# One product of states with C, issued as two operations with a signal each, in a hybrid attention, FFN and state-space kernel

## The reference, cut to what matters

```
def step(h, inputs):
    dt, bt, ct, xt_ = inputs
    decay = jnp.exp(A[None] * dt[:, :, None])
    inp = dt[:, :, None] * xt_[:, :, None] * bt[:, None, :]
    h = decay * h + inp
    y = jnp.einsum('bdn,bn->bd', h, ct)
    return (h, y)
```

## Time and profile before

| what | value |
| --- | --- |
| median of 3 runs | 1912.14 us (1906.36 to 1922.38) |
| profiled execution | 1914.16 us, with a span of 1912.4 us |
| granted TensorE clock, mean | 0.973 of full speed |
| busy: PE, DVE, ACT, POOL | 89%, 88%, 73%, 58% of the span |
| DMA engines | about 0.86 busy in a frame of the middle |

### The profile page before, as it was taken

The page is one execution under the profiler, slowest core; times in us unless marked ns, Lnnn a source line. Parts: engine busy times, 40 slices in busy tenths (PEclk is TensorE's granted clock), DMA queues, the critical chain, the costliest instruction groups (busy, mean ns, idle before and its releaser), DMA issues.

```text
span 1912.4 us, 31526 instructions
## 1 busy us (share of the span) xinstructions
PE 1704.7 (89%) x9578; PEld 1009.6 (53%) x9620; DVE 1678.1 (88%) x3928; ACT 1397.9 (73%) x2724; POOL 1117.4 (58%) x903
## 2 busy tenths in 40 slices
PE   6999788999989898999999898999999898888875
PEld 2555454646556564646555564646465564545333
DVE  5653889999999999999999999999999999977893
ACT  3666767797887978797887978787886968675541
POOL 2000565767667676767667676757667575766330
PEclk9999899999999999999999999999999999989998
DMA  5322586988879788979889787988878687761120
GB/s 144 91 59 75 118 170 137 186 159 169 166 148 193 153 183 149 192 159 170 165 158 185 156 186 151 184 159 176 156 161 182 144 172 145 149 128 50 55 62 11
DMA packets 216330, 275.30 MB, mean 144 GB/s; under 512 B 37169, under 2 KB 129122, under 8 KB 216162
## 3 DMA queue, kind: packets, MB, share of 16 engines
q1 hardware_dynamic: 155682, 163.17, 35.1%
q0 software_dynamic: 60480, 110.13, 34.8%
HBM read 128.49 MB, written 34.08 MB: 85 GB/s over the span
## 4 chain that ended last, share of the span: by engine, by line
PE 39%; DVE 23%; DMA 12%; issue 10%; POOL 9%; ACT 6%; SPq 1%; DVEq 0%; POOLq 0%; ACTq 0%
DVE hc L1274 10%; DMA y<-hc 8%; POOL inp L1448 6%; PE bank L422 5%; PE bank L624 5%; DVE bank L1130 4%; PE bank L541 4%; PE bank L641 3%; PE bank L486 3%; DVE hc L1282 3%; PE bank L508 3%; PE bank L625 2%; PE bank L433 2%; DMA sk<-qk_parts 1%; PE bank L604 1%
## 5 line engine op out<-in xcount | busy, mean ns | idle before, releaser
L1448 POOL TENSOR_TENSOR inp<-u,b_all 128x1024 f32<-128x1024 f32 x240 | 574.2, 2393 | 326.8 <-DVE hc L1274 123.1
L1274 DVE TENSOR_TENSOR_SCAN hc<-dec,inp 128x1024 f32<-128x1024 f32 x256 | 586.0, 2289 | 33.5 <-POOL inp L1448 13.4
L1130 DVE CUSTOM_DVE_ANT_0 bank<-bank,mask_qk 128x512 f32<-128x512 f32 (+3 forms) x1024 | 477.7, 508 | 77.8 <-PE bank L486 75.3
L915 ACT ACTIVATE pt<-bank 128x512 f32<-128x512 f32 x640 | 382.6, 608 | 108.1 <-PE bank L524 58.2
L1458 POOL DMA_DIRECT2D y<-hc x420 | 370.9, 954 | 132.8 <-DMA y<-hc 84.1
L1031 ACT ACTIVATE dec<-dt,a_neg 128x511 f32<-128x511 f32 x512 | 341.0, 732 | 70.2 <-DVE hc L1274 69.0
L1282 DVE TENSOR_TENSOR hc<-hc,bank 128x1024 f32<-128x1024 f32 x242 | 293.6, 1213 | 19.5 <-PE bank L678 18.6
L486 PE MATMUL bank<-sk,sq 96*128 96x512 bf16 (+3 forms) x1024 | 251.7, 307 | 36.1 <-DVE mall L1130 27.9
L508 PE MATMUL bank<-sq,sk 98*128 98x512 bf16 (+3 forms) x1024 | 250.6, 306 | 25.8 <-ACT pt L915 22.7
L541 PE MATMUL bank<-pt,v_sb 128*32 128x512 f32 (+3 forms) x2048 | 178.0, 453 | 1.8 <-ACT pt L915 1.7
L486 PEld LDWEIGHTS bank<-sk,sq 96*128 96x128 bf16 x1024 | 94.0, 99 | 147.7 <-issue 58.4
(11 more groups left out here) (169 smaller groups left out, 3024.0 us busy)
## 6 DMA issues: line engine op xcount, KB each, us to landing
y<-hc POOLq DMA_DIRECT2D x420, 256.0 KB, 4.7
b_all<-b_kept SPq DMA_DIRECT2D x256, 256.0 KB, 3.9
qk_parts<-parts SPq DMA_DIRECT2D x96, 256.0 KB, 3.0
sq<-qk_parts SPq DMA_DIRECT2D x384, 64.0 KB, 3.9
sk<-qk_parts SPq DMA_DIRECT2D x384, 64.0 KB, 4.0
X<-in_x SPq DMA_DIRECT2D x16, 512.0 KB, 5.9
out<-X SPq DMA_DIRECT2D x16, 512.0 KB, 4.0
sq<-hlt SPq DMA_DIRECT2D x256, 2.0 KB
```

What stands on the lines that cost most here:

```text
L915: A(pt[:, n % PT, :], score_bank[unit % 2][:, :], ACT.Exp).then_inc(exp_done.sem, 1)
L1130: return V.tensor_tensor_reduce(src[:, o:o + n], src[:, o:o + n], mask_qk[:, T - n:T], 1.0, -3.0e38, ALU.add, ALU.max, out)
L1274: V.tensor_tensor_scan(h, d, v, 0.0, ALU.mult, ALU.add).then_inc(scan_done.sem, 1)
L1448: G.tensor_tensor(inp[:, n % 2, :, :], u[:, :, :], b_all[:, k % 3, None, :].to_broadcast([P, C, T]), ALU.mult).then_inc(inp_ready.sem, 1)
```

## The change

`product` issues two VectorE operations, one for each half, in the places of its tables where the one stood. Each signals `hc_done`, which therefore counts two for each state. `add_state` waits for its own half's signal ahead of each DMA, and `sum_y` for its own half's ahead of each matmul. All other waits on `hc_done` (the spreading of C, and the scan that reuses the place of a state 0) are on both halves, as before.

```
-        hc_done = tally("products_with_c", NS)
+        hc_done = tally("products_with_c", C * NS)
...
-                pe.wait_ge(hc_done.sem, hc_done.at(s, n))
+                pe.wait_ge(hc_done.sem, hc_done.at(s, C * n))
...
-                    pe.wait_ge(hc_done.sem, hc_done.at(s, n + 1))
                     for c, m in enumerate(late_banks(s)):
+                        pe.wait_ge(hc_done.sem, hc_done.at(s, C * n + c + 1))
                         last = mm(m[:, :], ident[:, :], hc[:, (NS * s + n) % HC, c, :], start=(n == 0), stop=(n == NS - 1),
                                   skip_group_check=True)
...
-                    dve.wait_ge(hc_done.sem, hc_done.at(old_s, 1))
+                    dve.wait_ge(hc_done.sem, hc_done.at(old_s, C))
...
-                V.tensor_tensor(hc[:, k % HC, :, :] if n or s >= LATE else y[:, s % 2, :, :], hc[:, k % HC, :, :],
-                                spread_bank[:, None, :].to_broadcast([P, C, T]), ALU.mult).then_inc(hc_done.sem, 1)
+                for c in range(C):
+                    V.tensor_tensor(hc[:, k % HC, c, :] if n or s >= LATE else y[:, s % 2, c, :], hc[:, k % HC, c, :],
+                                    spread_bank[:, :], ALU.mult).then_inc(hc_done.sem, 1)
...
             def add_state(s, n):
-                pool.wait_ge(hc_done.sem, hc_done.at(s, n + 1))
                 for c in range(C):
+                    pool.wait_ge(hc_done.sem, hc_done.at(s, C * n + c + 1))
                     if n > 1:
                         pool.wait_ge(y_added[c].sem, y_added[c].at(s, n - 1))
```

## The result

| | kernel before | changed kernel |
| --- | --- | --- |
| median, 20 runs each | 1911.91 us (1906.36 to 1922.38) | 1920.13 us (1916.11 to 1924.20) |
| profiled execution | 1914.16 us, span 1912.4 us | 1922.31 us, span 1920.5 us |
| ratio of the runs | 1 | 1.004, 95% interval 1.003 to 1.005 |

The change makes the kernel slower by 0.4%: 8.2 us by the medians, 5.7 to 9.6 us by the interval of the ratio (0.003 and 0.005 times 1912). The interval doesn't reach 1.000, and all of it lies within the 1% that the prediction called no change. In the later experiments, four executions of the kernel before (2510 to 5977 us) and one of the version with 480 tokens (5120 us) stood far outside all the others, and no ratio uses them.

The account below looks back on a forecast made before the run. No engine alone holds the end; DVE is 96% busy in a frame, with some 4 us of slack. 6 (DVE) + 0.4 (POOL's wait) - 1.5 (POOL's earlier issue) - 0.7 (tail) = 4.2 us, so 1916 us; range 1905 to 1930.

Parts of the forecast that it names:

- DVE's price: Product on DVE: 0.05 us more each, 12.8 us over 256; two L1189 operations, writing in place, suggested the upper 0.07.
- How much reaches the end: Of DVE's added 12.8 us, between 2.8 (56 products in the chain) and all delays the end; half taken, 6 us.
- POOL's added wait: One more wait instruction on POOL in 210 places, 0 to 0.08 us each; 0.4 us slower taken.
- pairs of issues of 1.9 us and more: Sign against the prediction: POOL's paired DMA issues this long would mean its added wait costs visibly.
- POOL's earlier issue: POOL issues the first half's DMA earlier: 1.5 us gained, 0.5 from short waits and 1 from longer ones.
- my bound of 7.8: Most POOL time the earlier signal could save: 13 short waits at 0.05 us and 13 longer at 0.55.
- The tail: Last two batches on PE: the last sum starts earlier, and the last product's wait for C shrinks; 0.7 us gained.
- rival with DVE's cost in full: DVE bounds every frame, 0.07 us paid at all 256 products: 17.2 us slower, 1929 us; chance 0.17.
- the halves do not overlap: On DVE the second half starts only when the first ended: 0.15 us more per product, 1931 to 1950 us; chance 0.04.
- rival of a gain from earlier DMAs: The chain's accumulating DMAs start earlier and shorten the frame: 5.7 us faster, 1906 us; chance 0.14.
- DVE's busy time in a frame: Expected sign in the changed kernel's profile: a rise by about 0.8 us, to 103.5 or so.
- the 1 us that would have spoken against the prediction: Sign against the prediction: the frame, from one like event to the next, changes by more than 1 us.

Follow-up runs that it names:

- version with 480 tokens: Kernel before, one product operation over 480 of 512 tokens of each half, except state 0 of batches 0 to 13: ratio 0.9959, 7.8 us faster.
- kernels with two signals: Two product operations, each with its signal, against the kernel before: changed kernel run again 1.0044; with each wait for a half on both halves 1.0056.
- added waits alone: Kernel before with one product operation, plus waits on its signal ahead of each half's DMA or matmul: ratio 1.0000 (0.9987 to 1.0012).
- kernel with late waits: Changed kernel with both signals and all waits, but each wait for a half is on both halves: ratio 1.0056 to the kernel before.
- the one with one signal: Kernel before with two product operations, one signal after the second, and the old waits: ratio 1.0029, 5.5 us slower.
- late version: Kernel before with the change in the last two batches alone, whose products TensorE adds up: ratio 1.0011 (0.9996 to 1.0026).
- four operations, one signal: Kernel before with each product as four operations over 256 tokens of one half, one signal after the last, old waits: ratio 1.0055, 10.5 us slower.
- four operations, two signals: Four operations for each product, a signal after each half and the changed kernel's waits: ratio 1.0081 (1.0057 to 1.0104) to the kernel before.
- 384 tokens: Kernel before, one product operation over 384 of 512 tokens of each half, except state 0 of batches 0 to 13: ratio 0.9940, 11.5 us faster.

## Why the prediction was right, and where its sum was off

Forecast were 1916 us and 4.2 us more than before; measured were 1920.13 us and 8.2 more (5.7 to 9.6). The sign and the mechanism were right, and the terms are these:

- DVE's price. I took 0.05 us for a product, between 0.03 and 0.07. It is 0.064, near the end with the in-place form: 16.4 us and not 12.8.
- How much reaches the end. I took half, by judgment between a chain's share of 22% and all, so that it came near is in part luck. With 16.2 us taken off it was half, 7.8 us. With 16.4 added and nothing else it was a third, 5.5 us (2.9 to 8.2); the 8 to 11 us of the kernels with two signals hold whatever the signals cost as well. For 49 us added it was a fifth to a third, and for 64 us taken off less than a fifth. Half of the right dose is 8.2 us, where I had 6.
- POOL's added wait: 0.4 us expected, nothing measured in the time. The prediction named pairs of issues of 1.9 us and more as a sign that it was wrong. There were 65 such pairs of 210 already (from the first issue's start to the second's end); there are 107 and 103 in the two executions of the changed kernel, and 96 with the added waits alone, which is no slower. So the wait does cost POOL time, as the sign said, and POOL's idle time takes it up. As expected, none of the waits for a product stands ahead of the second half's DMA.
- POOL's earlier issue: 1.5 us expected, not resolved. The waits for the product fell by 8.7 us (21.4 to 12.7), about my bound of 7.8, but not as forecast: the short ones of 0.31 to 0.33 us are gone, and long ones are left (1.71 us where 2.0 to 2.3 stood, and 3.04 for 3.06). The waits for the DMA before rose by 19 us in the profiled execution and fell by 3 in the second one, so the 19 may be chance. Against the kernel with late waits some 2 us are won beside the tail, against the one with one signal 2 to 3 us are lost.
- The tail: 0.7 us expected, 0.67 seen in the changed kernel and 0.66 in its second run and in the late version; in the version with one signal it is absent (5.81 us from the last scan to the gating, against 5.75 before).

With the measured price, and my half kept, the sum is 8.2 + 0 - 0.7 = 7.5 us without POOL's gain and 6.0 with it, and both lie in the measured 5.7 to 9.6. But the half is not measured. With what the operations cost alone it is 5.5 - 0.7 = 4.8 us, and then some 3 us are left that no term of the prediction has; they could lie in the second signal or in the width of the intervals. So the price was too low by 0.014 us for each product, 2.2 of the 4.0 us that the forecast was short of if half passes, and for the rest POOL's gain or a cost of the signals is the suspect, not the proven cause. The rival with DVE's cost in full would have been 15.7 us, and is out. That the halves do not overlap is out as well: a half starts 0.60 us after the other at a duration of 0.68. The rival of a gain from earlier DMAs is out as a whole, since the changed kernel is slower; a small gain within the loss is not. Of the other signs, DVE's busy time in a frame rose by 0.5 and 0.9 us in the two executions (0.8 expected), and the frame grew by 0.7 and 0.4 us, less than the 1 us that would have spoken against the prediction.

The Trainium skill's "Vector Engine (DVE) Microarchitecture Reference", section 5.2, gave about 75 ns for an instruction after overlap. By the trace, each one added cost 64 ns, twice over (1.133, 1.197 and 1.326 us for one, two and four). Its "VectorE: DVE Perf Modes" says in the section on the errata that small tiles pay for each instruction what a large one pays once; the trace agrees. The same page's section "The DRAIN you can't avoid", as the prediction quotes it, lets the next operation start only when the pipeline is empty; but it goes on that one that is not held starts earlier. The trace agrees with the second sentence: the second half starts 0.08 us before the first ends.

What stays open: whether the operations beyond the second really cost less in proportion than the first one added, which the ratios say and a comparison at equal clock doesn't (last section). Open too is whether the second signal in itself costs 3 to 5 us. Single executions of one kernel differ by 3 us in the middle, and six to twelve runs do not settle it.

## What to carry to other kernels

Splitting an operation so that a follower starts earlier costs the fixed part of an instruction at each place (0.064 us on VectorE here), and pays only where that follower waits for it and nothing else ends later; count those places first, since here only the last of 256 showed a gain in the trace. An engine that is 96% busy may still pass only a third to a half of an added cost; price a small change by experiments of about the same size with either sign, since a large relief (64 us here) passed less than a fifth. One profiled execution shows the price of an operation well, to a few ns, but where a loss of 0.4% sits can't be read from it: set executions of versions without the change beside it first, and look at the granted clock of the stretch. A wait that gets shorter (POOL's for the product, by 8.7 us) need not show in the time.

## What the runs showed of the hardware

The scatter of the runs follows the granted TensorE clock. Of 22 runs of the kernel before in one set, the fastest, 1905.95 us, had a mean granted clock of 0.982, and the slowest, 1921.29 us, 0.970. A line fitted through the 208 runs whose clock is on record (without the five far outside), with a level of its own for each kernel and one slope for all, gives 0.93 us less for each 0.001 of clock: 11 of the 15 us between those two.

With a level for each set of runs as well, and the same slope, the differences to the kernel before at equal clock are these, with 95% intervals:

| version | us, at equal clock |
| --- | --- |
| two operations, one signal | 5.0 (3.2 to 6.8) |
| one operation, added waits | 1.7 (-0.1 to 3.5) |
| changed kernel, run again | 8.3 (6.2 to 10.4) |
| two signals, late waits | 9.4 (7.3 to 11.5) |
| four operations, one signal | 14.3 (12.3 to 16.3) |
| four operations, two signals | 17.2 (14.8 to 19.6) |
| change in the last two batches alone | 2.5 (0.8 to 4.2) |
| change in the first fourteen alone | 7.6 (5.9 to 9.3) |
| 480 tokens | -6.1 (-8.4 to -3.8) |
| 384 tokens | -8.7 (-11.0 to -6.4) |

Two things look otherwise here than by the ratios. The added operations pass the same share at both doses, 0.30 of 16.4 us and 0.29 of 49. And the second signal with its waits costs 4.4 us (1.6 to 7.2) from the two operations with one signal to those with late waits, of which the waits may be 1.7. This is a fit made after the fact, and the granted clock may itself depend on the version, as in the trace of the four operations; so it is a leaning, not a proof.
